# Small-head attentions: the division by the softmax sums moved from TensorE and ScalarE to 32x32 blocks on VectorE

## The reference

```
x = x + attn_a(norm(x))        16 heads of 8 channels, softmax, with a norm of q and k
x = x + local(norm(x))         6 layers of windowed attention (16 heads of 64) and feed-forward
x = x + attn_b(norm(x))        16 heads of 8 channels, latent q, k, v, causal softmax
x = x + local(norm(x))         the same weights again
x = x + linear(norm(x))        out = q' (k'^T v) / (q' sum(k') + 1e-8), q' and k' of 32 features a head
x = x + feed_forward(norm(x))  gate, up, silu, down, 384 wide
x = x + attn_c(norm(x))        16 heads of 8 channels, causal softmax
x = x + feed_forward(norm(x))
```

## Time and profile before

| | |
|---|---|
| median of three executions | 4467.09 us |
| the profiled execution | 4461.44 us |
| its span, first to last instruction | 4459.6 us |
| TensorE matmuls (PE) busy | 4152.4 us, 93% |
| TensorE weight loads (PEld), beside the matmuls | 2055.3 us, 46% |
| VectorE (DVE) busy | 3384.6 us, 76% |
| ScalarE (ACT) busy | 2976.2 us, 67% |
| GpSimd (POOL) busy | 2310.6 us, 52% |
| granted TensorE clock, mean, as a share of 2.4 GHz | 0.978 |

### The profile page before, as it was taken

How to read it: one execution, slowest core, us unless ns; L and a number is a source line. 1 busy time by engine, 2 the same in 40 slices (tenths; PEclk the granted TensorE clock), 3 DMA queues, 4 the chain that set the end, 5 groups by cost and what they waited for, 6 DMA issues and landing times. The chain is left out here.

```text
span 4459.6 us, 129030 instructions
## 1 busy us (share of the span) xinstructions
PE 4152.4 (93%) x54074; PEld 2055.3 (46%) x54074; DVE 3384.6 (76%) x5176; ACT 2976.2 (67%) x7393; POOL 2310.6 (52%) x1450
## 2 busy tenths in 40 slices
PE   5898999999999999998989999999999999978896
PEld 2222555555555455553435555554555545534442
DVE  3774888888888888885758888888888888844762
ACT  2665777777777777774557777777777777756553
POOL 3202766666666666663016666666666666621100
PEclk8999999999999999998999999999999999989998
DMA  5112000000000000002120000000000000000110
GB/s 169 44 39 53 2 21 7 2 21 7 21 7 2 21 7 2 2 3 67 52 63 2 12 17 2 21 7 21 7 2 21 7 2 2 2 14 31 56 33 8
DMA packets 69399, 98.08 MB, mean 22 GB/s; under 512 B 34440, under 2 KB 59236, under 8 KB 62820
## 3 DMA queue, kind: packets, MB, share of 16 engines
q1 hardware_dynamic: 67956, 83.54, 6.3%
q10 hardware_dynamic: 864, 6.29, 0.3%
HBM read 72.44 MB, written 16.78 MB: 20 GB/s over the span
## 5 line engine op out<-in xcount | busy, mean ns | idle before, releaser
L402 POOL TENSOR_TENSOR ra<-ra,rb 128x1024 f32<-128x1024 f32 x384 | 927.5, 2415 | 327.4 <-DVE rb L741 327.4
L416 POOL TENSOR_TENSOR qkr<-ra,inv 128x1024 f32<-128x1024 f32 x384 | 731.5, 1905 | 608.0 <-ACT inv L680 604.3
L448 PE MATMUL ps<-wvo,xs 128*32 128x512 f32 x6144 | 822.9, 607 | 70.8 <-ACT vs L602 70.8
L493 PE MATMUL ps<-wq,xs 128*128 128x512 f32 x1536 | 743.2, 606 | 7.3 <-DVE rb L741 4.5
L653 ACT ACTIVATE pr<-ps,neg 128x64 f32<-128x64 f32 x3072 | 670.3, 338 | 7.1 <-DVE neg L718 7.1
L602 ACT ACTIVATE vs<-ps 128x512 f32<-128x512 f32 x768 | 451.3, 588 | 225.4 <-PE ps L448 224.1
L515 PEld LDWEIGHTS ps<-kt,qt 64*32 64x32 f32 x24576 | 360.3, 107 | 294.0 <-issue 289.6
L718 DVE TENSOR_REDUCE neg<-ps 128x8 f32<-128x512 f32 x384 | 263.7, 687 | 284.0 <-PE ps L515 277.1
L1475 DVE TENSOR_REDUCE nm<-ps 128x1 f32<-128x512 f32 (+3 forms) x768 | 378.4, 547 | 126.6 <-PE ps L1243 124.9
L493 PEld LDWEIGHTS ps<-wq,xs 128*128 128x128 f32 x1536 | 272.4, 190 | 429.5 <-issue 332.9
L738 DVE TENSOR_TENSOR ra<-ps,rope 128x1024 f32<-128x1024 f32 x384 | 451.7, 1176 | 21.0 <-ACT sq L627 14.1
(11 more groups left out here) (261 smaller groups left out, 6355.0 us busy)
## 6 DMA issues: line engine op xcount, KB each, us to landing
wq<-in_L_ffn_Wqkv SPq DMA_DIRECT2D x12, 1024.0 KB, 5.1
wvo<-wvo_scratch SPq DMA_DIRECT2D x12, 1024.0 KB, 5.0
wvo_scratch<-pt ACTq DMA_DIRECT2D x6, 1024.0 KB, 4.0
w<-in_L_ffn_W SPq DMA_DIRECT2D x12, 341.0 KB
qs<-norm_pieces SPq DMA_DIRECT2D x9, 384.0 KB
ks<-norm_pieces SPq DMA_DIRECT2D x9, 384.0 KB
qs<-latent_pieces SPq DMA_DIRECT2D x9, 384.0 KB
ks<-latent_pieces SPq DMA_DIRECT2D x9, 384.0 KB
```

The source lines that it names most:

```text
L402: pool.tensor_tensor(ra[:, m % 2, :, :], ra[:, m % 2, :, :], rb[:, :, :], ALU.add).then_inc(sum_done.sem, 1)
L416: pool.tensor_tensor(qkr[:, m % 2, :, :].rearrange("p s (h c) -> p (s h) c", c=HD), ra[:, m % 2, :, :].rearrange("p s (h c) -> p (s h) c", ...
L448: last = pe.matmul(VP[32 * j:32 * j + 32, :], xs[:, turn % 2, v * WIN:v * WIN + WIN], wvo[l % 2][:, j, :], start=True, stop=True)
L493: last = pe.matmul(PJ[:, qk, :], xs[:, turn % 2, t * P:t * P + P], wq[l % 2][:, at:at + 512], start=True, stop=True)
```

## The change

For the three small attentions and the linear attention:

- `sums`, its load, the product with it, Ln, Exp and the full-length multiplication are gone, with their semaphores.
- One step after `ou` is kept, VectorE transposes `ou` in 32x32 blocks into `turned`: tokens go to partitions, and each block has its head's 8 channels and the sum (column 8) beside each other. It takes the reciprocal of that column for the 16 blocks (`rd`, 128x16), and multiplies the 8 channels of each block by it into columns 8g to 8g+7 of the blocks of `compact`. After the fourth group `compact` holds all 16 heads' channels and is transposed back into `on`, 128 channels by 512 tokens.
- One output product for a batch, two steps earlier, with `wp` of 128x128, its rows ordered as (head in group, group, channel). `wp` is loaded whole and no longer cleared by GpSimd.
- Each small attention and the linear attention have two steps fewer; the last batch of the last feed-forward starts at its step 46.
- In the linear attention the 1e-8 is added when `ou` is kept (Identity with a bias column loaded from `sum_floor`).

The tiles `out` (whose first part is `on`), `rd` and the smaller `wp` take the places of `rr`, `on` and the larger `wp`. The diff, cut to its core (the linear attention's part repeats the small attention's with its own steps):

```diff
-        "sum_rows": np.kron(np.eye(4), np.outer(np.arange(32) == SD, np.ones(32))).astype(np.float32),
+        "sum_floor": (1e-8 * (np.arange(P) % 32 == SD))[:, None].astype(np.float32),
...
-    rows = w.rearrange("(g j c) m -> j c g m", g=SG, j=4)
+    rows = w.rearrange("(g j c) m -> j g c m", g=SG, j=4)
     for j in range(4):
-        sp.dma_start(wp[32 * j:32 * j + SD, :, :], rows[j]).then_inc(sem, 16)
+        sp.dma_start(wp[32 * j:32 * j + 32, :], rows[j]).then_inc(sem, 16)
+
+
+def normed_at(g, i):
+
+    return 3 * g + g // SG + i
+
+
+NORMED = 3 * SG + 1
...
-    FIRST, LAST = PLAIN_FIRST if kind == "plain" else -SH - 11, ROW_ITEMS + LAG + 10
+    FIRST, LAST = PLAIN_FIRST if kind == "plain" else -SH - 11, ROW_ITEMS + LAG + 8
...
-    rr = heads_only("rr", [P, 2, SEQ])
-    on = heads_only("on", [P, SG, SEQ])
+    out = heads_only("out", [P, 4, SEQ])
+    rd = heads_only("rd", [P, SEQ // 32])
     mcut = (heads_only if kind == "plain" else side)("mcut", [4 * TB, 2, PARTS, P], BF16)
-    sums = side("sums", [P, P])
-    wp = side("wp", [P, SG, P])
+    wp = side("wp", [P, P])
     ou = (heads_only if kind == "plain" else side)("ou", [P, 2, SEQ])
     qs, ks = (qs0, qs1), (ks0, ks1)
+    on = out[:, 0, :]
+    turned, compact = (out[:, 1 + i, :].rearrange("p (t c) -> p t c", c=32) for i in range(2))
...
             if kind == "latent" and k == 0:
-                sp.wait_ge(prep_pool.sem, prep_pool.at(3))
-                sp.dma_start(sums[:, :], d["sum_rows"]).then_inc(ld_w.sem, 16)
+                local.attention_free(sp)
+                local.z_final(sp, BATCH - 1)
                 load_output_weights(core, sp, wp, d[f"{n}_W_o"], ld_w.sem)
...
-                    if (before := group_at(k, 13)) is not None:
-                        pe.wait_ge(ln_done.sem, ln_done.at(before + 1))
-                        if before % SG == SG - 1:
-                            pe.wait_ge(added.sem, added.at(before // SG + 1))
+                    if (before := group_at(k, 13)) is not None and before % SG == SG - 1:
+                        pe.wait_ge(added.sem, added.at(before // SG + 1))
...
-            if (g := group_at(k, 10)) is not None:
-                pe.wait_ge(out_kept.sem, out_kept.at(g + 1))
+            if (g := group_at(k, 10)) is not None and g % SG == SG - 1:
+                pe.wait_ge(out_normed.sem, out_normed.at(normed_at(g, 4)))
                 pe.wait_ge(mcut_done.sem, mcut_done.at(6 * min(g + 3, ROW_GROUPS - 1) + 1))
-                pe.matmul(ps[:, MISC_BANK, :], sums[:, :], ou[:, g % 2, :], start=True, stop=True).then_inc(sum_mm.sem, 1)
-            if (g := group_at(k, 12)) is not None and g % SG == SG - 1:
-                pe.wait_ge(out_normed.sem, out_normed.at(g + 1))
-                for gg in range(SG):
-                    last = pe.matmul(ps[:, MISC_BANK, :], wp[:, gg, :], on[:, gg, :], start=gg == 0, stop=gg == SG - 1)
-                last.then_inc(y_mm.sem, 1)
+                if g == SG - 1:
+                    pe.wait_ge(ld_w.sem, ld_w.at(16 * n_ld))
+                pe.matmul(ps[:, MISC_BANK, :], wp[:, :], on, start=True, stop=True).then_inc(y_mm.sem, 1)
...
-                    act.wait_ge(out_normed.sem, out_normed.at(g - 1))
+                    act.wait_ge(out_normed.sem, out_normed.at(normed_at(g - 2, 1)))
                 act.activation(ou[:, g % 2, :], ps[:, AV_BANK, :], ACT.Copy).then_inc(out_kept.sem, 1)
...
-            if (g := group_at(k, 10)) is not None:
-                act.wait_ge(sum_mm.sem, sum_mm.at(g + 1))
-                act.activation(rr[:, g % 2, :], ps[:, MISC_BANK, :], ACT.Ln).then_inc(ln_done.sem, 1)
-                act.wait_ge(ln_done.sem, ln_done.at(g + 1))
-                act.activation(rr[:, g % 2, :], rr[:, g % 2, :], ACT.Exp, scale=-1.0).then_inc(recip_done.sem, 1)
...
-            if (g := group_at(k, 11)) is not None:
-                dve.wait_ge(recip_done.sem, recip_done.at(g + 1))
-                if g >= SG:
-                    dve.wait_ge(y_mm.sem, y_mm.at(g // SG))
-                dve.tensor_tensor(on[:, g % SG, :], ou[:, g % 2, :], rr[:, g % 2, :], ALU.mult).then_inc(out_normed.sem, 1)
-            if (g := group_at(k, 12)) is not None and g % SG == SG - 1:
+            if (g := group_at(k, 9)) is not None:
+                dve.wait_ge(out_kept.sem, out_kept.at(g + 1))
+                if g:
+                    dve.wait_ge(out_normed.sem, out_normed.at(normed_at(g, 0)))
+                dve.transpose(turned.rearrange("p t c -> p (t c)"), ou[:, g % 2, :]).then_inc(out_normed.sem, 1)
+                dve.wait_ge(out_normed.sem, out_normed.at(normed_at(g, 1)))
+                dve.reciprocal(rd[:, :], turned[:, :, SD]).then_inc(out_normed.sem, 1)
+                dve.wait_ge(out_normed.sem, out_normed.at(normed_at(g, 2)))
+                dve.tensor_tensor(compact[:, :, SD * (g % SG):SD * (g % SG) + SD], turned[:, :, 0:SD],
+                                  rd[:, :, None].to_broadcast([P, SEQ // 32, SD]), ALU.mult).then_inc(out_normed.sem, 1)
+                if g % SG == SG - 1:
+                    dve.wait_ge(out_normed.sem, out_normed.at(normed_at(g, 3)))
+                    if g >= SG:
+                        dve.wait_ge(y_mm.sem, y_mm.at(g // SG))
+                    dve.transpose(on, compact.rearrange("p t c -> p (t c)")).then_inc(out_normed.sem, 1)
+            if (g := group_at(k, 10)) is not None and g % SG == SG - 1:
                 b = g // SG
                 dve.wait_ge(y_mm.sem, y_mm.at(b + 1))
                 dve.tensor_tensor(x[:, cols_of(b)], x[:, cols_of(b)], ps[:, MISC_BANK, :], ALU.add).then_inc(added.sem, 1)
...
@@ linear_attention
-            b, g = part_at(k, 12, SG)
-            if b is not None:
-                if b == 0 and g == 0:
+            if (b := batch_at(k, 13)) is not None:
+                if b == 0:
                     pe.wait_ge(ld_wp.sem, ld_wp.at(64))
-                pe.wait_ge(out_normed.sem, out_normed.at(SG * b + g + 1))
-                last = pe.matmul(ps[:, KV_BANK, :], wp[:, g, :], on[:, g % 2, :], start=g == 0, stop=g == SG - 1)
-                if g == SG - 1:
-                    last.then_inc(y_mm.sem, 1)
-            b, g = part_at(k, 10, SG)
-            if b is not None:
-                pe.wait_ge(out_kept.sem, out_kept.at(SG * b + g + 1))
-                if g:
-                    pe.wait_ge(recip_done.sem, recip_done.at(2 * (SG * b + g) - 1))
-                pe.matmul(ps[:, SUM_BANK, :], sums[:, :], ou[:, g % 2, :], start=True, stop=True).then_inc(sum_mm.sem, 1)
+                pe.wait_ge(out_normed.sem, out_normed.at(NORMED * (b + 1)))
+                pe.matmul(ps[:, KV_BANK, :], wp[:, :], on, start=True, stop=True).then_inc(y_mm.sem, 1)
...
-                act.activation(ou[:, g % 2, :], ps[:, g % 2, :], ACT.Copy).then_inc(out_kept.sem, 1)
+                    act.wait_ge(out_normed.sem, out_normed.at(normed_at(SG * b + g - 2, 1)))
+                act.activation(ou[:, g % 2, :], ps[:, g % 2, :], ACT.Identity, bias=cols[:, 1:2]).then_inc(out_kept.sem, 1)
...
+            b, i = part_at(k, 9, SG)
             if b is not None:
-                dve.wait_ge(recip_done.sem, recip_done.at(2 * (SG * b + g) + 2))
-                dve.tensor_tensor(on[:, g % 2, :], ou[:, g % 2, :], rr[:, g % 2, :], ALU.mult).then_inc(out_normed.sem, 1)
-            if (b := batch_at(k, 15)) is not None:
+                g = SG * b + i
+                dve.wait_ge(out_kept.sem, out_kept.at(g + 1))
+                if g:
+                    dve.wait_ge(out_normed.sem, out_normed.at(normed_at(g, 0)))
+                dve.transpose(turned.rearrange("p t c -> p (t c)"), ou[:, i % 2, :]).then_inc(out_normed.sem, 1)
+                dve.wait_ge(out_normed.sem, out_normed.at(normed_at(g, 1)))
+                dve.reciprocal(rd[:, :], turned[:, :, SD]).then_inc(out_normed.sem, 1)
+                dve.wait_ge(out_normed.sem, out_normed.at(normed_at(g, 2)))
+                dve.tensor_tensor(compact[:, :, SD * i:SD * i + SD], turned[:, :, 0:SD],
+                                  rd[:, :, None].to_broadcast([P, SEQ // 32, SD]), ALU.mult).then_inc(out_normed.sem, 1)
+                if i == SG - 1:
+                    dve.wait_ge(out_normed.sem, out_normed.at(normed_at(g, 3)))
+                    dve.transpose(on, compact.rearrange("p t c -> p (t c)")).then_inc(out_normed.sem, 1)
+            if (b := batch_at(k, 13)) is not None:
...
-    STARTS = (0, 14, 28, 42) if first else (0, 14, 28, 50)
+    STARTS = (0, 14, 28, 42) if first else (0, 14, 28, 46)
```

More of the change, by code:

```diff
@@ L1549, in small_attention @@
     prep_pe.leave(2 if kind == "plain" else 0)
-    prep_pool.leave(4 if kind == "norm" else 3)
+    prep_pool.leave(2)
     ld_low.leave(16 * loads * BATCH)
@@ L1606, in linear_attention @@
     own = tile("own", [P, P])
-    sums = tile("sums", [P, P])
     cols = tile("cols", [P, 2])
```

85 lines of the change are left out of this document (31 added, 54 removed).

## The result

The changed kernel takes 4424.91 us (median of 4 executions, 4423.4 to 4432.5) against 4466.93 us before; the ratio is 0.9913, with a 95% interval from 0.9896 to 0.993. Forecast were 4387 us, 80 us less; measured are 42 us less. The sign is right, the size is not: half of the gain is missing.

A forecast was written before the change was run, and what follows sets the result against it. Small attention groups were taken as bound by TensorE's queue, VectorE having slack. Gains of 20.1, 23.4 and 20.4 us (64 together) plus 16 in the linear attention gave 80: 4387 us as a median; 8 in 10 range 4358 to 4430.

The forecast's parts named there:

- rival 4: TensorE, less busy, is granted a lower clock: 42 us on top outside the local block, gain 38, 4429 us; 5%.
- the walk through the group: Unmasked group: fourth score some 1.2 us later, removed matmul gives 0.96 back, exponentials some 0.6 earlier; net gain 0.6 us.
- 13 x 0.6: Unmasked stage's sum: 13 groups at 0.6 us gain, beside 3 x 1.7 for batch ends and 7.2 for its end; 20.1.
- rival 1: VectorE becomes the bound: regular groups gain nothing, batch ends, stage ends and half the linear stage leave 43 us, 4424; 17%.
- Division on VectorE 1.28 us: A group's division: transpose 0.70, reciprocal 0.20, strided multiplication 0.28, waits 0.1 us; the last group of a batch 2.0.
- Masked group, 0.9 taken: Masked attention group gains 0.96 us plus part of the stall behind ScalarE; 0.9 taken, bounds 0.3 and 1.5.
- Unmasked group, 0.6 taken: Unmasked attention group, now 14.7 us, gains 0.6 net, to about 14.1; bounds 0 and 1.7.
- End of a batch: Batch ends about 1.6 us longer than other groups instead of 3.3 to 3.5; gains 1.7 unmasked, 1.9 masked.
- End of a stage: Chain from `ou` to the adding shrinks from 7.6 to 3.9 us; whole ends gain 7.2 unmasked, 6.0 masked.
- Latent and last attention: Masked stages gain 23.4 us and 20.4 us, the last being the same less an estimated 3.0 for the feed-forward's chain.
- Rival 3: Slower: the division holds VectorE's queue over 2.5 us a group; at 3.0 it is 30 us slower, 4497; 4%.
- the prediction's other case (all three held): GpSimd could hold transpose, reciprocal and multiplication, catching 13% of 48 instructions about 1 us each: 6 us less gain per attention.

The follow-up runs named there:

- wait filled: Changed kernel with an unread 128x128 by 128x512 f32 product put into TensorE's wait, ahead of the fourth score, in the first attention; 4402.16 us.
- product outside: Changed kernel with an unread product of the sum product's size put back in its old place in the first attention; 4438.86 us.
- two steps late: Changed kernel with the small attentions' division, output product and adding two steps later, the last group staying; 4377.48 us.
- unread product: Kernel two steps late, with an unread product of the sum product's size in its old place in all four attentions, 64 in all; 4404.58 us.
- added wait: Kernel before, with two VectorE transposes of 128x512 f32 added in the first attention where the changed kernel divides; 4493.35 us.
- one step late: Changed kernel with the small attentions' division, output product and adding one step later, the last group staying; 4384.9 us.
- half of the wait: Kernel two steps late, with the group's transpose alone put back between the cuts and the reductions; 4388.29 us.
- four output products: Kernel two steps late, with each batch's output product made four times over in the small attentions and the linear one; 4407.88 us.

## Why the prediction was wrong

**The step that failed** is the price of the lower clock, rival 4. The prediction took the clock as a function of how busy TensorE is over a stage, read a line from three rows, got 2 us a stage from it, and put no term for the clock into the sum of the unmasked stage. That line says nothing of where the idle time lies. The change put 1.3 us of it in one piece into every unmasked group, and the clock fell to 1.2 GHz for about 7 us of the group (a clock of 0.80 over 17.3 us; the stretch from 334.0 to 340.3 has 0.57, where 0.5 would be all of it at 1.2). In the last seven groups this cost some 17 us, against a forecast that had nothing for it. I had this wait in the walk through the group ("that score comes some 1.2 us later") and set the removed 0.96 us against it as if the two were of one kind. In time they nearly are, 14.3 us at the full clock against 14.1 forecast; for the clock they are not. The first attention in parts, in us, by the starts of its heads (the last seven groups have a clock of 1.00 in the kernel before):

| | before | forecast | after | wait filled | product outside | two steps late |
|---|---|---|---|---|---|---|
| heads 0 to 3 | 8.1 | 8.1 | 8.1 | 8.1 | 8.1 | 8.1 |
| first eight groups, heads 3 to 35 | 134.8 | 130.7 | 140.4 | 146.4 | 152.2 | 139.5 |
| last seven, heads 35 to 63 | 107.2 | 102.8 | 122.0 | 104.5 | 122.4 | 93.4 |
| from head 63 to the last adding | 61.2 | 50.0 | 54.2 | 52.7 | 56.2 | 52.8 |

The forecast is spread over these parts as follows. Five divisions fall among the first eight groups, four of them ordinary ones (0.6 each) and one a batch end (1.7): 134.8 - 4.1 = 130.7. The last seven are seven groups of 14.1 us, with 1.6 more at each of the two batch ends that lie among them now and 0.9 for the group that keeps the values, as before: 102.8. Before the change the third batch's output products came behind head 63 (338.24 in the earlier trace rows; the head starts at 336.2), now they come ahead of it. So their 3.4 us leave the last part, beside the 0.6 of one more group and the 7.2 of the stage's end: 61.2 - 11.2 = 50.0.

All three parts came out longer than forecast, by 9.7, 19.2 and 4.2 us. The last seven groups are explained. With the wait filled they are 17.5 us shorter than in the changed kernel: that is the clock. With the division two steps late they are another 11.1 shorter: that is the lateness of the score, 1.2 in each of five groups and 2.9 and 2.0 at the two batch ends, where the adding has moved too. So of 28.6 us that these groups lose against the division two steps late, some 17 are the clock's and some 11 the late score's own. The last part was shortened by 7.0 us, which looks like the forecast's 7.2 but contains the 3.4 of the batch end that moved out. The chain in it came out 3.0 shorter (7.6 to 4.6) where 3.7 were forecast, at a clock of 0.72 against 0.87 before; the rest of its miss is not taken apart. The first eight groups stay open.

A slip in the sum is small beside this: 13 x 0.6 takes in groups 13, 14 and 15, which the end of the stage counts again, 1.8 us too much in the first stage and 2.7 in each of the masked ones.

That the total of 4425 lies next to rival 1 (4424) and rival 4 (4429) is half luck. Rival 1's sign was groups that keep 14.7 and 11.5 us; at the full clock they don't. Rival 4 named the cause and direction, at 5%, but spread it over all stages; it struck above all the first (0.95 to 0.84, the masked ones 0.96 to 0.94 and 0.95). The Trainium skill, "TensorE: Matmul & The Clock Gate", "What's actually happening", was quoted there for the clock as granted by recent activity, and the clocks here agree with it in direction: 0.80 with the wait empty, 0.90 with a product behind it, 1.00 with a product in it. I should have asked of each added wait what TensorE does during it, not only how long the stage is idle.

**Point by point.**
- Division on VectorE 1.28 us: 1.24 and three waits of about 0.03. Right. The strided multiplication is close to the lower bound (0.292 against 0.28); the reciprocal of 16 elements takes 0.253, not 0.20.
- Masked group, 0.9 taken: 11.5 to 10.3 is 1.2. With the division two steps late 10.0, the upper bound of 1.5; the product is 0.9 of it (10.9 with the unread product); the other 0.6 is left for ScalarE's Ln and Exp, which no run took away alone.
- Unmasked group, 0.6 taken: 14.7 to 14.3 is 0.4 at the full clock, and 1.6 with the division two steps late (bound 1.7). The product is 0.9 of it; 0.7 is left for Ln and Exp, close to the 0.74 that TensorE waited in the earlier trace rows.
- End of a batch, 1.6 us longer than other groups: in the masked stages 1.1 and 2.1 (groups of 11.4 and 12.4). The adding is not covered: at the second batch's end in the first attention VectorE stood 3.21 us waiting for the product, with the next reductions behind it. In the unmasked stage the excess is 1.7 to 2.4 us over groups that are themselves slowed.

```profile
287.16 0.69 DVE L1500 TENSOR_TENSOR x<-x,ps 128x512 f32<-128x512 f32 x1 [3.21 <-PE ps L1312]
```

- End of a stage, from `ou` to the adding, 3.9 us against 7.6: 4.6; the last product takes 1.84 us, mostly at 1.2 GHz (a clock of 0.58 over it), in a stretch with a clock of 0.72:

```profile
408.12 0.60 ACT L1395 ACTIVATE ou<-ps 128x512 f32<-128x512 f32 x1 [2.25 <-PE ps L1303]
...
410.87 1.84 PE L1312 MATMUL ps<-out,wp 128*128 128x512 f32 x2 [2.82 <-DVE out L1496]
...
412.75 0.69 DVE L1500 TENSOR_TENSOR x<-x,ps 128x512 f32<-128x512 f32 x1 [1.93 <-PE ps L1312]
```

- Latent and last attention: -19.1 and -24.0 against -23.4 and -20.4; linear -13.1 against -16. Right within 5 us each, from terms that were each a little off.
- The local blocks kept their length within 1 us. The preparation took 2.7 us more, at a clock of 0.77 in its first 86 us instead of 0.93. The runs do not tie it to the change or to that clock: the kernel before with the added wait took 88.8 us at 0.93, and the kernels with the changed kernel's preparation took 87.0 to 89.6, at 0.93 or 0.94 in five and 0.76 to 0.78 in three.
- Rival 3, slower, from 2.5 us a group on: the division held VectorE's queue for 1.3 us, at a batch end 2.0. But the first attention did get slower, by another way than the one named.

**What stays open.** The first eight groups of the unmasked attention run at a lower clock in the kernel before too (groups of 12.8 to 20.0 us), and here the versions scatter: the same code took the stage 293.8 and 287.9 us in two kernels. They took 134.8 us before, 140.4 after, 146.4 with the wait filled, 139.5 and 133.6 in those two, 136.8 one step late, 135.6 with half of the wait, 136.7 with the unread sum products and 129.3 with four output products. No run separates the reasons; only the last of these shows a gain of the size forecast (4.1), and it has more work than its neighbours. Nor is it shown why one wait of 1.32 us in seven left the clock alone, or why 1.38 us behind an idle product did. The stages' lengths are from one execution each (of the kernel two steps late it was the slowest of four, 4389.05), so differences of a few us between stages are not safe; the medians are.

## What to carry to other kernels

When a change takes work from TensorE and gives a neighbour work that TensorE must wait for, price the wait twice: by its length, and by the clock behind it. Look for the step in which the receiving engine waits for TensorE anyway and put the new work there; here two steps later was worth 47 us. If there is no such step, independent work inside the wait keeps the clock; behind the wait it wins back half of it here and pays only for itself. Small removals from a TensorE that is nearly full return less than their busy time: 58 us of products taken away were worth 27.

## What the runs showed of the hardware

- A single wait of TensorE of 1.3 us in a group of 14 us in which it is otherwise nearly always busy was followed by the clock at 1.2 GHz in six of seven groups, and two of 1.06 us in another kernel too; one of 0.67 in a group of 13.7 was not, in any of the last seven groups of that run. A product of 1.02 us in the wait, leaving 0.46, kept the clock as well, and at batch ends even with 1.38 and 1.17 left. The same product behind the wait raised the clock of the group from 0.80 to 0.90.
- VectorE's multiplication of two tiles was held during GpSimd's subtractions, its transpose and reciprocal were not. In the linear attention the multiplication's median is 0.292 us, but these two took 1.50 and 1.76, to just after the end of a GpSimd subtraction (L1138 to 4112.73, L1142 to 4116.03); transpose and reciprocal that overlap the same subtractions took their usual time (0.71 and 0.70, 0.25 and 0.26). The Trainium skill, "SBUF — State Buffer", "Who interferes with whom", says so of instructions with two SBUF inputs and with one; the trace agrees, and the prediction's other case (all three held) is out. In the three small attentions none of the 48 multiplications was held (291 to 294 ns).

```profile
4110.61 2.12 POOL L1138 TENSOR_TENSOR x<-xf,cut 128x1024 f32<-128x1024 f32 x1
...
4113.91 2.12 POOL L1142 TENSOR_TENSOR x<-x,cut 128x1024 f32<-128x1024 f32 x1
```

```profile
4111.09 0.25 DVE L1791 RECIPROCAL rd<-out 128x16 f32<-128x16 f32 x1
4111.38 1.50 DVE L1793 TENSOR_TENSOR out<-out,rd 128x128 f32<-128x128 f32 x1
...
4113.40 0.70 DVE L1789 STREAM_TRANSPOSE out<-ou 128x512 f32<-128x512 f32 x1
4114.13 0.26 DVE L1791 RECIPROCAL rd<-out 128x16 f32<-128x16 f32 x1
4114.42 1.76 DVE L1793 TENSOR_TENSOR out<-out,rd 128x128 f32<-128x128 f32 x1
```
